# Mean passes of a graph network run as one sequence of 26 quads, with the sorted edge records placed by matrix products

## The reference, cut to what matters

```python
# layer 0: two graph convolutions; layer 1: two weighted means; layer 2: a symmetric degree-scaled sum
for Qw, Qb, Ww, Wb in params:                       # layer 1
    h_q = leaky_relu(h @ Qw.T + Qb)
    h_agg = segment_sum(h_q[src] * w[:, None], dst) / segment_sum(w, dst)[:, None]
    h_new = leaky_relu(concat([h, h_agg], 1) @ Ww.T + Wb)
    h = h_new / norm(h_new, axis=1)
# layer 2: sums over edges of dinv[row] * dinv[col] * x[col], and of x*x
# layer 3: messages = relu(relu([x_i, x_j - x_i] @ W1 + b1) @ W2 + b2), summed over edges by target, / degree
```

## Time and profile before

| | us |
|---|---|
| median of 3 runs | 4312.65 (4310.07 to 4320.18) |
| the profiled execution's own time | 4315.21 |
| its span in the trace | 4313.4 |
| PE busy | 3622.9 (84%) |
| DVE busy | 2969.4 (69%) |
| POOL busy | 1864.6 (43%) |
| ACT busy | 1680.0 (39%) |
| mean granted clock of TensorE | 0.921 |

### The profile page before, as it was taken

The page is one execution under the profiler, slowest core; times in us unless marked ns, Lnnn a source line. Parts: engine busy times, 40 slices in busy tenths (PEclk is TensorE's granted clock), DMA queues, the critical chain, the costliest instruction groups (busy, mean ns, idle before and its releaser), DMA issues.

```text
span 4313.4 us, 90312 instructions
## 1 busy us (share of the span) xinstructions
PE 3622.9 (84%) x36043; PEld 2714.0 (63%) x36044; DVE 2969.4 (69%) x5334; ACT 1680.0 (39%) x5041; POOL 1864.6 (43%) x1803
## 2 busy tenths in 40 slices
PE   7888888898887778888477786798889999999997
PEld 6888888888876653333222332598666666666665
DVE  8999999999877752444444444244667767777676
ACT  4888888888878840000000000000222222222222
POOL 1000000000000001577777777700777777777775
PEclk9999999999989989998688887799999999999998
DMA  3777777777866679999699999796444444444444
GB/s 145 290 288 293 296 277 293 280 294 288 314 213 228 225 252 380 334 287 288 157 260 260 285 257 294 180 390 233 116 118 121 118 120 119 122 117 120 116 124 93
DMA packets 431793, 969.03 MB, mean 225 GB/s; under 512 B 80335, under 2 KB 356585, under 8 KB 406025
## 3 DMA queue, kind: packets, MB, share of 16 engines
q1 hardware_dynamic: 371497, 899.18, 61.7%
q0 software_dynamic: 59872, 64.00, 7.9%
HBM read 641.05 MB, written 321.95 MB: 223 GB/s over the span
## 4 chain that ended last, share of the span: by engine, by line
POOL 29%; DVE 27%; PE 22%; issue 11%; ACT 8%; DMA 3%; POOLq 0%; DVEq 0%; ACTq 0%; SPq 0%
POOL recs_d L1955 16%; POOL e_rows L1979 13%; DVE tab L635 10%; ACT stream L2011 6%; DVE hot_s L632 5%; PE acc L2613 4%; DVE tab L630 4%; PE acc L2674 3%; PE acc L2685 2%; PE acc L2642 2%; PE acc L2580 2%; PE acc L2649 1%; PE acc L991 1%; PE acc L2660 1%; DMA stream<-w_d 1%
## 5 line engine op out<-in xcount | busy, mean ns | idle before, releaser
L1979 POOL DMA_INDIRECT e_rows<-parts_d,e_gidx x980 | 963.1, 983 | 505.0 <-issue 294.1
L1955 POOL DMA_INDIRECT recs_d<-recs,places_i x735 | 798.6, 1087 | 223.9 <-issue 223.9
L2580 PE MATMUL acc<-stream,tab 128*64 128x512 f32 (+1 forms) x2548 | 666.6, 619 | 59.0 <-DMA stream<-w_d 57.5
L889 PE MATMUL acc<-tab,hot_s 128*128 128x196 bf16 x3136 | 619.8, 249 | 68.2 <-DVE tab L635 31.5
L891 PE MATMUL acc<-tab,hot_s 128*128 128x98 bf16 x3136 | 585.4, 210 | 5.4 <-issue 5.4
L892 PE MATMUL acc<-tab,hot_s 128*128 128x98 bf16 x3136 | 584.3, 210 | 2.3 <-issue 2.3
L635 DVE TENSOR_TENSOR tab<-tab,weights 128x2352 bf16<-128x2352 bf16 x392 | 540.3, 1378 | 0.0
L784 ACT CAST a_line<-acc 128x392 bf16<-128x392 f32 x784 | 472.1, 602 | 125.7 <-PE acc L892 109.8
L2580 PEld LDWEIGHTS acc<-stream,tab 128*64 128x64 f32 x2548 | 203.1, 148 | 445.6 <-issue 378.0
L557 POOL DMA_INDIRECT fetch<-edges_in,row_of x50 | 67.0, 1341 | 956.7 <-DVE row_of L571 948.8
L784 ACT COPY w_half<-acc 128x392 f32<-128x392 f32 x784 | 474.8, 606 | 0.0
(11 more groups left out here) (284 smaller groups left out, 6797.5 us busy)
## 6 DMA issues: line engine op xcount, KB each, us to landing
stream<-w_d SPq DMA_DIRECT2D x168, 1792.0 KB, 21.1
w_d<-w_half SPq DMA_DIRECT2D x98, 1568.0 KB, 9.4
a_d<-a_line SPq DMA_DIRECT2D x49, 1568.0 KB, 5.8
stream<-a_d SPq DMA_DIRECT2D x49, 1568.0 KB, 6.8
stream<-at_d SPq DMA_DIRECT2D x84, 896.0 KB, 16.5
e_lowT<-recs_d SPq DMA_DIRECT2D x126, 448.0 KB
at_d<-at_runs SPq DMA_DIRECT2D x49, 896.0 KB, 4.1
at_d<-at_runs SPq DMA_DIRECT2D x49, 640.0 KB
```

Of the source, the lines that this page charges most:

```text
L889: mm(to, s, cols[:, 0:2, :].rearrange("p a n -> p (a n)"), start=k % 2 == 0, stop=True, skip_group_check=True)
L1955: pool.indirect_dma_start(recs_d, bass.IndirectOffsetOnAxis(places_i[:, i % 2, t:t + 1], 0), recs[:, i * TPB + t, :], None, bounds_check=S ...
L1979: pool.indirect_dma_start(e_rows[:, i % GRING, t, :], None, parts_d, bass.IndirectOffsetOnAxis(e_gidx[:, i * EG + t:i * EG + t + 1], 0)).t ...
L2580: last = mm(to[s % 2 * D:(s % 2 + 1) * D], table[:, s, :], wide_pieces[:, i % WIDE_SLOTS, 0:cols, :, d * P // 2:(d + 1) * P // 2], start=s ...
```

## The change

It does three things.

1. The two mean passes become one run of 26 quad steps (`RUN`). The work behind a part is spread: DVE's norms in step n if the part was whole with quad n-1 (`normed_beside`), its turn, q and dense products on PE in step n+1 (`turned_beside`), one chunk a piece. The last part of CONV2, MEAN1 and MEAN2 is done behind pieces 2 to 5 of the first quad of what follows (`last_part`), and that quad waits for the new table piece by piece (`table_in`), not for all of it.
2. Records of sorted blocks are no longer scattered by POOL. DVE makes one-hots of a record's tile (50 columns, times its two numbers) and of its slot in the tile (128 columns) in `make_places`, for 7 tiles at a time; PE multiplies them (`sort`, 35 products of 100 x 128 per block, summed in bank 5); ACT copies the result with the pad value as bias, and stores it (`lay_records`, 100 rows of 256 bytes). `rank` is two narrow products per block, `take_ranks` is three wide operations. The fill of `recs_d` with pads goes.
3. The stores of `store_ends` move from SP to ACT. `WIDE_SLOTS` goes from 6 to 5 and `PIECE_SLOTS` from 12 to 10, to make room. The layout of `recs_d` puts the two numbers of a record apart, so that the EDGE stage loads two runs per group and PE reads them side by side; their load for `s_low2` is one transfer and 21 products, where it was nine and nine.

```diff
-STREAMS, PIECE_SLOTS, WIDE_SLOTS = 4, 12, 6
+STREAMS, PIECE_SLOTS, WIDE_SLOTS = 4, 10, 5
-        recs_d = dram("recs_d", [S_SLOTS, 2], BF16)
+        recs_d = dram("recs_d", [len(S_BLOCKS), 2, STILES, P], BF16)
...
+        RUN = 2 * QUADS
+        PIECE_OF_SORT = 3
+        SORT_OF = {n: i for i, n in enumerate(n for n in range(RANKS_FROM, RUN) if n != QUADS)}
+        def normed_beside(n):
+            return whole_by(n - 1)
+        def turned_beside(n):
+            part = whole_by(n - 2)
+            return None if part is None or part[1] == NBANK - 1 else part
...
             for i in range(2 * WIDES):
                 load_weights(i)
-                step, j = divmod(i - WIDE_SLOTS, PIECES)
-                c = step - ENDS_FROM - 2
-                if j == 3 and 0 <= c < ECH:
-                    store_ends(c)
...
         def gpsimd_dense(pool):
-            def put_records(i):
-                pool.wait_ge(places_made, i + 1)
-                for t in range(TPB):
-                    pool.indirect_dma_start(recs_d, ..., recs[:, i * TPB + t, :], ...)
...
+            def lay_records(i):
+                act.wait_ge(places_used, S_EG * (i + 1))
+                if i >= 2:
+                    act.wait_ge(placed[i % 2], 16 * (i // 2))
+                nc.scalar.activation(recs_t[0:2 * STILES, i % 2, :], bank(5)[0:2 * STILES, P:2 * P], ACT.Identity,
+                                     bias=pad_low[0:2 * STILES, :]).then_inc(recs_laid, 1)
+                act.wait_ge(recs_laid, i + 1)
+                act.dma_start(recs_d[i].rearrange("k s e -> (k s) e"), recs_t[0:2 * STILES, i % 2, :])\
+                    .then_inc(placed[i % 2], 16)
+            for n in range(1, RUN + 1):
+                copy_sums(n - 1)
+                normed, turned_now = normed_beside(n), turned_beside(n)
+                if turned_now:
+                    turn_nodes(*turned_now)
+                if n - 1 in SORT_OF:
+                    lay_records(SORT_OF[n - 1])
+                if normed:
+                    part_roots(*normed)
...
+                if 0 <= n - ENDS_FROM - 1 < ECH:
+                    store_low(n - ENDS_FROM - 1)
+                if 0 <= n - ENDS_FROM - 2 < ECH:
+                    store_ends(n - ENDS_FROM - 2)
...
+            def take_ranks(i):
+                counts = so_far[:, 1:].rearrange("p (b t) -> p b t", t=TPB)
+                dve.wait_ge(ranked, i + 1)
+                node(v.tensor_tensor(counts, counts, bank(5)[:, 0:BLOCKS].unsqueeze(2).to_broadcast([P, BLOCKS, TPB]),
+                                     ALU.add))
+                node(v.tensor_tensor(counts, counts, in_block[:, :, :], ALU.mult))
+                node(v.tensor_reduce(ranks, counts.rearrange("p b t -> p t b"), AX.X, ALU.add))
+            def find_slots(i):     # eight small operations on 35 to 140 columns
+            def make_places(i, q):
+                n, tiles = i * S_EG + q, slice(q * EG, (q + 1) * EG)
+                if n >= SRING:
+                    dve.wait_ge(places_used, n - SRING + 1)
+                node(v.tensor_tensor(in_tile ..., ramp_b[:, 0:STILES] ..., slot2[:, 0, tiles, :] ..., ALU.is_equal))
+                v.tensor_tensor(by_tile[:, n % SRING ...], in_tile ..., low_less[:, tiles, :, :] ..., ALU.mult)
+                node(v.tensor_tensor(in_slot[:, n % SRING ...], ramp_b ..., slot2[:, 1, tiles, :] ..., ALU.is_equal))
+                v.engine_nop().then_inc(places_made, 1)
...
+            def sort_beside(n, normed, turned_now):
+                # order: mean_begin, take_ranks, mean_end, find_slots, places 0, q, places 1, q,
+                # last_norm_begin, places 2, last_norm_end, table, places 3, table, places 4
+            for n in range(1, RUN + 1):
+                take_quad(n - 1)
+                if n % QUADS == 0:
+                    last_part(whole_by(n - 1)[0])
+                else:
+                    sort_beside(n, normed_beside(n), turned_beside(n))
...
+                elif n in SORT_OF and SORT_OF[n] + 1 < len(S_BLOCKS):
+                    mark_tiles(SORT_OF[n] + 1)
+                if 0 <= c < ECH:
+                    tile_ends(c)
...
+            def rank(i):
+                pe.wait_ge(tiles_marked, i + 1)
+                if i >= 1:
+                    pe.wait_ge(recs_laid, i)
+                mm(bank(5)[:, 0:BLOCKS], parts_before[:, :], ends_of, start=True, stop=False)
+                mm(bank(5)[:, 0:BLOCKS], up_to_less[:, :], starts_of, start=False, stop=True).then_inc(ranked, 1)
+            def sort(i, q):
+                n = i * S_EG + q
+                pe.wait_ge(places_made, n + 1)
+                for t in range(EG):
+                    last = mm(bank(5)[0:2 * STILES, P:2 * P],
+                              by_tile[:, n % SRING, t, :, :].rearrange("p k s -> p (k s)"), in_slot[:, n % SRING, t, :],
+                              start=q == 0 and t == 0, stop=q == S_EG - 1 and t == EG - 1)
+                last.then_inc(places_used, 1)
+            def table_in(p, j):
+                pe.wait_ge(dense_out, CHUNKS * (LAYER[p] - 1) + 2 * (j + 1))
+            for n in range(RUN):
...
+                for j in range(PIECES):
+                    if g == 0:
+                        table_in(p, j)
...               # the piece's loads and products as before
+                    if j == 0 and n > 0:
+                        turn_sums(n - 1)
+                    if g == 0 and 2 <= j <= 5:
+                        last_part(CONV2 if n == 0 else MEAN1, j)
+                    if turned_now:   # part_turn at j 0, one q at j 2 and 3 (MEAN1), one dense at j 4 and 5
+                    if j == 2 and 0 <= n - ENDS_FROM - 1 < ECH:
+                        turn_ends(n - ENDS_FROM - 1)
+                    if j == 0 and n - 1 in SORT_OF:
+                        sort(SORT_OF[n - 1], S_EG - 1)
+                    if j == 1 and i_sort is not None:
+                        rank(i_sort)
+                    if j >= PIECE_OF_SORT and i_sort is not None:
+                        sort(i_sort, j - PIECE_OF_SORT)
```

More of the change, by code:

```diff
@@ L315, in build @@
         prep = tab[:, 1, BLOCKS * ROW:]
-        pads = pairs_d[:, :, :, :].rearrange("p a b f -> p (a b f)").bitcast(BF16)[:, 0:2 * S_TILES]
+        ranks, places, apart = (ranking[:, k, :] for k in range(3))
+        d_first = ranking[:, :, :].rearrange("p a t -> p (a t)")[:, 0:BLOCKS]
         ends = prep[:, 0:2 * P].rearrange("p (a e) -> p a e", a=2)
@@ L2034, in scalar_dense, with turn_nodes, part_q @@
             roots(DEGREE_ROOT_D)
-            for p in (MEAN1, MEAN2):
-                for g in range(QUADS):
-                    copy_sums(p, g)
-                    if g in PART_OF:
-                        part_roots(p, PART_OF[g])
-                        part_turn(p, PART_OF[g])
+            def turn_nodes(p, k):
+                for c in (2 * k, 2 * k + 1):
+                    scalar_turn(act, LAYER[p], c)
+            def part_q(p, k):
+                if p in (CONV2, MEAN1):
+                    for c in (2 * k, 2 * k + 1):
+                        scalar_q(act, LAYER[p], c)
@@ new lines, in sort_beside @@
+            def sort_beside(n, normed, turned_now):
+                i = SORT_OF.get(n)
+                q0, q1 = ((LAYER[turned_now[0]], 2 * turned_now[1] + k) for k in range(2)) if turned_now else (None, None)
+                with_q = turned_now and turned_now[0] == MEAN1
+                if normed:
+                    mean_begin(normed[1])
+                if i is not None:
+                    take_ranks(i)
+                if normed:
+                    mean_end(*normed)
+                if i is not None:
+                    find_slots(i)
+                    make_places(i, 0)
+                if with_q:
+                    vector_q(dve, *q0)
+                if i is not None:
+                    make_places(i, 1)
+                if with_q:
+                    vector_q(dve, *q1)
+                if normed and normed[0] == MEAN2:
+                    last_norm_begin(normed[1])
+                if i is not None:
+                    make_places(i, 2)
+                if normed and normed[0] == MEAN2:
+                    last_norm_end(normed[1])
+                if turned_now:
+                    table_chunk(*q0)
+                if i is not None:
+                    make_places(i, 3)
+                if turned_now:
+                    table_chunk(*q1)
+                if i is not None:
+                    make_places(i, 4)
@@ L2616, in tensor_dense_path @@
                     last.then_inc(piece_used, 1)
+                    if g == 0 and j == 0:
+                        turn_sums(RUN - 1)
+                        sort(SORT_OF[RUN - 1], S_EG - 1)
+                    if g == 0 and 2 <= j <= 5:
+                        last_part(MEAN2, j)
+                    if g == 1 and j == 0:
+                        pe.wait_ge(mean_taken, RUN)
                     k = PART_OF.get(g - 1)
```

379 lines of the change are left out of this document (179 added, 200 removed).

## The result

The changed kernel takes 4091.1 us (median of 4 runs, 4084.0 to 4102.6) against 4314.2 us beside it: a ratio of 0.948, 95% interval 0.9454 to 0.9507, or 223 us less. The forecast was 4040, so 51 us of the predicted gain of 272 are missing. The profiled execution took 4096.7 us, its span is 4093.7. Every measured time of a kernel is the median of its fast runs; one run of z4 (5688.7 us) was slow and is left out.

The account below looks back on a forecast made before the run. The weight stream `w_d`, slowed by record scatters, was taken as the bound, plus border losses. Start 1571, quads 910 and end 16 give 2497 against 2769, 272 us less: 4040; forecast 4010 to 4075, range 3975 to 4130.

Parts of the forecast that it names:

- my sign of being right: In the profile after, 370 GB/s or more through the mean passes, with no record scatter.
- The price of a record: Mean passes: each scattered record costs 43 ns of one DMA engine, 253 us of the whole DMA for 94080.
- Nineteen sorted quads of 37.3: Mean passes: 19 full quads with sorting at 37.3 us each, 709 us.
- the coupling: DMA, PE and DVE waiting on each other in a sorted quad: between 34.5 and 42 us, taken as 37.3.
- Two small quads of 14: Ends of MEAN1 and MEAN2: 14 us charged for each small quad, 28 together, as five slots fill meanwhile.
- Tail and BY_SRC: 16 us charged for the end of MEAN2; BY_SRC itself changes by 0, at most 5 us.
- EDGE: as before: EDGE stage as long as before, 1295 us from 3018 to the end; the new record layout gives nothing.
- The sixth slot: Weight loads: cover falls from 24 to 19 us with five slots; costed at nothing.
- A: Rival: coupling costs more, sorted quads of 42 us, 89 us more, 4130; chance 0.21 for 4075 to 4150.
- B: Rival: coupling almost free, 34.5 to 35 us a quad, 45 to 53 us less, 3990; chance 0.20.
- C: Rival: DMA rate stays at 288 GB/s, 4247 us; chance 0.09 with whatever keeps part of the loss.
- D: Rival: DVE-PE hand-over paces quads, slower above 51.6 us each; at 56 us, 4395; chance 0.03.

Follow-up runs that it names:

- z4: Kernel before with 21 of each block's 35 record scatters left, waits set to match, second kind of chip: 4608.8 us, ratio 0.9228.
- y3: Changed kernel with PE's sort products one piece later and edge work one step earlier, last small quad sorting nothing, first kind of chip: 4015.3 us, ratio 0.9302.
- y2: Changed kernel with the 735 scatters put back into a spare tensor at even places, first kind of chip: 4178.2 us, ratio 0.9677.
- y1: Kernel before without the 735 record scatters and the waits for them, first kind of chip: 4192.6 us, ratio 0.9721.
- x4: Changed kernel without sorting in the two small quads, second kind of chip: 4363.1 us, ratio 0.8751.
- y0: Changed kernel itself, unaltered, run again on the first kind of chip: 4091.9 us, ratio 0.9471.
- x3: Changed kernel with PE's sort products one piece later, second kind of chip: 4314.9 us, ratio 0.8669.
- x2: Changed kernel with the 735 scatters put back into a spare tensor, second kind of chip: 4923.2 us, ratio 0.9887.
- z1: Kernel before with its record scatters sent to even places of a spare tensor, second kind of chip: 4984.4 us, ratio 0.9999.
- z2: Changed kernel with 735 scatters to sorted places in a spare tensor, 26 between two fetches, second kind of chip: 4929.8 us, ratio 0.9878.
- z3: Changed kernel with 735 scatters to even places, 26 between two chunks' fetches, the rest behind the last, second kind of chip: 4920.6 us, ratio 0.988.

## Why the prediction was right or wrong

**What bounds the kernel.** The stream of `w_d` at 381 GB/s as the floor holds: y3 comes within 35 us of it. That the scatters lowered the rate in the kernel before holds too: taken out, 346 GB/s for 288 (290 in the same 185 us). But my sign of being right, 370 GB/s or more, was not met by the changed kernel (363 and 338): there the hand-over and the small quads held the stage, not the DMA.

**The price of a record, 43 ns of one DMA engine, fell.** I took the whole lost rate of one stretch and divided it by the records. It is no price of a record as such: in y2 as many per microsecond left the stream at 378 GB/s. And it is no time that records take on an engine: q0, with the fetches in it, is 3.4% of the 16 engines and not 24%. It was also no measure of time: I called it 253 us of the DMA, and the kernel got 119 back, with DVE's 96.5 us of waits for the scatters, which I had not priced, gone as well. The sum didn't use the 253 us directly. It used 34.5 us of DMA per quad beside PE's and DVE's, and so came out near: that the rate would come back was right, the reason for it was not.

**The other half.** The predicted 272 us less did not say how they divide, and the division depends on what goes first. Scatters first: 119 for them (y1), then 101 for the rest of the change. The rest first: 133 for it with scatters kept, into the spare tensor (y2, 4311.5 to 4178.2), then 86 for them. In y1 the DMA is idle for a fifth of its time behind the old order; in y2 POOL's queue is in the way of the new one.

**The sum, term by term** (predicted, then measured in the profile):
- Start and four unsorted quads: 4.8 + 138 = 143; 150.4, from 1575.0 to 1725.4. The 7 us more are all in the first quad: PE begins 7.4 us behind the first load and not 4.8, and works 39.1 us to the turn of sums for 34.5, with the last part of CONV2 between its pieces (0.9 us idle at most at a time).
- Nineteen sorted quads of 37.3: 709; 696.2 (291.1 + 405.1), 36.6 each. The value between 34.5 and 42 that I took for the coupling was 13 us too high in all.
- The unsorted quad behind the border: 34.5; 38.6.
- **Two small quads of 14: 28; 68.1.** This is the term that failed, 40 us of the 51. "The small quad 12 still carries a whole DVE step (about 30 us) over 8.6 us of load, but the five slots fill meanwhile": they do, but full slots give back nothing where PE is busy 33.2 to 33.6 us of each full quad itself (365.22/11, 268.88/8). What DVE takes longer there, less PE's own work, is lost for good. x4 shows it: without sorting the same quads are 18.3 and 21.2 us, on the other kind of chip but with large quads of the same length.
- Tail and BY_SRC: 16 + 228 = 244; 244.1, from 2528.3 to 2772.4. (I read BY_SRC's end off the chain as 3018 us. Its last product starts at 2997.1; at 3018 the last piece of `parts_d` is stored. The sum doesn't use it.)
- First load: 9 us later. In y0, the same kernel, it is at 1586.0, in y3 at 1566.2, so this is spread.
- EDGE: as before; 4.5 us more from the first gather on (1292.1 before, 1296.6 after, and 1292.1 again in y0 and y3). The new rows of the records gave nothing, as charged.

9 + 7 - 13 + 40 + 4 = 47 us up to the end of the mean passes, and 4.5 behind: 51. The 13 us too many for the coupling hid part of the miss; without them it would be 64 us, still inside the range.

**The costs of the parts.** DVE per sorted quad was 28.8 to 29.1 us (230.62/8, 319.57/11), for 31.4. PE's 35 sort products were 0.55 to 0.59 us for seven at the full clock, 2.9 a quad as predicted, and 0.98 at the lower. The three stores of a chunk on ACT landed in 5.1 to 5.9 us (medians; 17.7 for `low_b` on SP) and nothing waited for them. The sixth slot was not tried by itself.

**The rivals.** A (42 us a quad) has the mechanism: PE's waits for one-hots are the dearest in the stage, 71.5 us, and the piece behind one is at the lower clock. Its size was wrong, 36.6 and not 42. B, 35 a quad, is what one more piece of distance gives (x3: 35.0 and 33.2). C is out: 363 and 338 GB/s. D would have needed 51.6 us a quad. On the second kind of chip D's figure is reached, but by the scatters, in kernels that have them (x2: 60.8 and 54.1 us a sorted quad).

The Trainium skill ("DMA: Bandwidth & Descriptors", section "Where 436 GB/s comes from") puts the limit of a core's loads from HBM at about 358 GB/s, which it works out as half of a stack's 716 for two cores; this kernel runs on one. No run here is held to it: the 381 of the earlier trace rows came again as 380 or 381 in every run (377 on average over 370 us in y3), so the measurement decides.

## What to carry to other kernels

A lost rate divided by the events beside it is a price only where the same events, put beside the same stream elsewhere, cost the same; a run with them put back shows it, and a run without them shows what is late next. Where one engine hands to another inside a step, put a full unit of work between the making and the reading: two constants gave 77 us here, 65 of them seen in the stage, nearly as much as the 86 of all the scatters put back. Before charging an engine for small transfers, look at what their own queue takes of it: here 3.4%, where the lost rate said 24%. A short unit that carries a whole step of side work is as long as the side work, however full the buffers are, if the main engine has no slack.

## What the runs showed of the hardware

**Engines that stand while POOL scatters.** On the second kind of chip, z1, instructions of POOL, ACT and PE around the end of a row of 35 scatters (start, length, work, idle before):

```profile
1809.92 0.97 POOL L1956 DMA_INDIRECT spare_d<-recs,places_i  x1 [0.30 <-issue]
1811.20 0.97 POOL L1956 DMA_INDIRECT spare_d<-recs,places_i  x1 [0.30 <-issue]
1811.96 0.59 ACT L2022 COPY sumsT<-acc 128x512 f32<-128x512 f32 x1 [57.61 <-issue]
1812.60 1.97 PE L2567 MATMUL acc<-two_idents,sumsT 128*128 128x64 f32 x8 [20.82 <-issue]
1816.86 0.52 DVE L2291 TENSOR_TENSOR own_count<-in_block,acc 128x343 bf16<-128x343 bf16 x1 [30.99 <-remote]
```

The scatters began at 1767.66 and their last at 1811.20. PE's last products end at 1791.8, and from there on ACT has nothing that it waits for. It goes on at 1811.96, and the others behind it. SP, which issues the loads, has no row between these two:

```profile
1784.31 3.95 SPq L1861 DMA_DIRECT2D stream<-w_d  x1
1811.95 0.36 SPq L1861 DMA_DIRECT2D stream<-w_d  x1
```

The rate in forty parts from 1775 to 1960 us:

```profile
GB/s 383 382 378 393 360 46 0 0 247 346 392 252 309 131 0 310 124 0 7 342 49 0 12 371 18 302 337 376 380 278 34 377 24 256 142 0 0 0 143 257
```

It is mostly near 380 or near nothing: the loads that are out are finished by about 1800 us, and none follows while SP and PE stand. Stretches at or near zero are in x2, z2 and z3 too. In z4, with two fifths of the scatters gone, the rate falls to 68 to 105 at times, but not to zero, and three quarters of the 507 us are gone. On the first kind y2 has no such stretch from 1775 to 1960 us. What the engines lack is not shown.

**The gathers of EDGE** take longer there too, in every kernel (1524 to 1549 us from first to last in the eight, 1261 to 1266 in the runs of the first kind): the 980 gathers of z1 (second kind), and of y3 (first), first and last start:

```profile
L1980 POOL DMA_INDIRECT e_rows<-parts_d,e_gidx x980: 939/947/1544, 3380.3 to 4915.5; - x196
```

```profile
L1990 POOL DMA_INDIRECT e_rows<-parts_d,e_gidx x980: 940/944/1508, 2721.0 to 3982.3; - x196
```

1535 us against 1261, with nearly the same median for one (947 and 944 ns). A kernel whose stage leans on POOL's indirect transfers has two times, by the chip that it falls on, and taking them off POOL is worth far more on one than on the other.
